# Layer-norm statistics of a transformer block with experts: finishing them once per stage instead of once per tile

## The chip, the cores and the metric

The kernel runs on all 8 cores of one Trainium2 chip. Each core takes half of one of four sequences, 2048 tokens, and does the whole computation for them; the cores exchange nothing. The metric is the device time in microseconds (us) of the slowest core.

## The reference

x has shape (4, 4096, 1024). What is computed, cut to what matters:

```python
h = layernorm(x) * (1 + ca) + sa               # sa, ca, ga, sb, cb, gb from silu(c) @ wmod
a = layernorm(h) * ln1_w + ln1_b
q, k, v = a @ qkv_w.T                          # 16 heads of 64
x1 = h + local_attention(q, k, v) @ proj_w.T   # block of 128 and both neighbours
z = layernorm(x1) * ln2_w + ln2_b
s2 = x + ga * (x1 + gelu(z @ fc1_w.T) @ fc2_w.T)
h2 = layernorm(s2) * (1 + cb) + sb
y = s2 + gb * experts(h2)                      # 8 experts, the best 2 by gate
```

A layer norm needs two numbers per token: the reciprocal standard deviation, and minus the mean times it.

## The kernel before

It is one program of direct engine instructions: every engine has a queue of its own, written in program order, and waits on semaphores by hand (`E.wait`; `waitr` waits relative to the stage's start, `wdma` for a labelled DMA). Tiles are 128 tokens by 1024 features; a core owns 16. The stages follow one another with a barrier between them, at which every engine drains:

1. Modulation vectors from `wmod` (to 227 us of the profile).
2. Two layer norms, the q, k and v projections (to 805).
3. Attention, the output projection, the first residual (805 to 1415). It writes x1, and the residual basis `s_sxa`, to memory and keeps the statistics of x1 in `stats_ln2`, two columns per tile.
4. The MLP (1415 to 2182): 8 groups of two tiles. It reads `stats_ln2`, writes s2, and keeps the statistics of s2 in `stats_s2`.
5. Routing and loading of the experts' weights (to 2447), then the experts (to the end).

**Statistics.** `emit_lnstats` (L233) is called at the end of each tile in stages 3 and 4. VectorE sums the row (L239), ScalarE squares it with an accumulated output (L241, which the trace shows as an ACTIVATE and an accumulator read). Then follow, on columns of one element: VectorE's mean (L245), its square (L250), the variance (L253), plus eps (L257); ScalarE's Ln (L261) and Exp with scale -0.5 (L264); VectorE's product (L268). Each waits for the one before.

**Order in an attention tile.** For each head TensorE makes the scores (L876), ScalarE the exponential with its row sum (L889), TensorE three transposes (L826), VectorE copies them (L831), TensorE multiplies with v (L844). Transposes are written one head behind the scores and the v products two; head 0's transposes wait until two exponentials are done. After 16 heads come the transposes of the output (L909), the projection in two bursts of 8 matmuls (L920) with a bias (L924), VectorE's residual sums (L932, L934, L944, L948) and the statistics. TensorE goes on to the scores of the next tile at once.

**Order in an MLP group.** TensorE runs fc1 in 32 pieces of 8 matmuls (L1143), ScalarE applies gelu to each (L1151), and fc2 (L1122) follows one piece behind. At the end `prep_tile` normalises the next two tiles (L1085 on ScalarE, L1093 and L1097 on VectorE, transposes L1103, copy L1110). Then for each of the group's two tiles VectorE scales the fc2 output (L1174, L1177), adds the residual (L1181), and the statistics follow. The next group's fc1 waits for both tiles' L1181, since it frees the output banks. In the attention and the MLP stage squaring writes its unused result into scratch: `sq_tr2` in attention, `u2_buf` in the MLP, and L1174 writes into `u2_buf` too:

```python
E.wait("tensor", SZTE, SZTE.n)
waitr("tensor", SS2, 2 * g)          # L1134: both tiles of the group before have their sum
```

Of the kernel before, what the change touches and what calls it, by code (L numbers as in the profile page):

```python
# [7 lines left out]
F32 = mybir.dt.float32  # L8
# [8 lines left out]
NT_OWN = 16  # L17
# [67 lines left out]
def build_program(taps=(), nphases=6, a2_tiles=NT_OWN, a2_nopf=99):  # L85
# [633 lines left out]
    if nphases == 2:  # L719
# [16 lines left out]
    ssum = A.alloc("ssum", [128, HEADS], F32)  # L736
    rrb = A.alloc("rrb", [128, HEADS], F32)
    sq_tr2 = A.alloc("sq_tr2", [128, D], F32)
    smA2 = {k: A.alloc(f"smA2_{k}", [128, 1], F32) for k in
            ("s1", "mu", "mu2", "varb", "var", "lnv")}  # L740

    LKVs = [mkdma(f"LKV{i}") for i in range(4)]
    LVVs = [mkdma(f"LVV{i}") for i in range(4)]
# [42 lines left out]
    for t in range(min(NT_OWN, a2_tiles)):  # L786
# [131 lines left out]
        for n in range(2):  # L918
            for k in range(8):
# [44 lines left out]
    if nphases == 3:  # L964
# [166 lines left out]
    for g in range(8):  # L1131
        tiles = (2 * g, 2 * g + 1)
        E.wait("tensor", SZTE, SZTE.n)
        waitr("tensor", SS2, 2 * g)  # L1134
        for m in range(32):
            mu = g * 32 + m
            fb = 2 + (mu % 2)
            if g == 0:
                waitr("tensor", WCM, 8 * (m // 4) + 8)
            waitr("tensor", SGE, mu - 1)  # L1140
            for k in range(8):
                E.op("tensor", lambda e, kk=k, mm=m, b=fb, zt=zT_gr[g % 2]:
                     e.matmul(  # L1143
                         bf(b)[:, 0:256],
                         wfc1_bf[:, kk * DFF + mm * 128: kk * DFF + mm * 128 + 128],
                         zt[:, kk * 256:(kk + 1) * 256],
                         start=(kk == 0), stop=(kk == 7)),
                     inc=SF1.bump() if k == 7 else None)
            E.wait("scalar", SF1, SF1.n)
            waitr("scalar", SF2C, mu - 1)  # L1150
            E.op("scalar", lambda e, mm=m, b=fb, st=tT_r[mu % 2]: e.activation(  # L1151
                st[:, :], bf(b)[:, 0:256], AF.Gelu, bias=fc1b_fm[:, mm:mm + 1]),
                inc=SGE.bump())
            if m >= 1:
                emit_fc2(g, m - 1)
        emit_fc2(g, 31)
        for lt, t in enumerate(tiles):
            ob = obA if lt == 0 else obB
            if g == 0 and lt == 0:
                waitr("tensor", WCB, 1)  # L1160
            for n in range(2):
                E.op("tensor", lambda e, nn=n, b=ob[n]: e.matmul(
                    bf(b)[:, :], ones_bf[0:1, 0:128],
                    fc2b_bf[0:1, nn * 512:(nn + 1) * 512],
                    start=False, stop=True),
                    inc=SF2T.bump() if n == 1 else None)
        if g + 1 < 8:
            prep_tile(2 * g + 2, (g + 1) % 2, 0)
            prep_tile(2 * g + 3, (g + 1) % 2, 1)
        for lt, t in enumerate(tiles):  # L1170
            ob = obA if lt == 0 else obB
            E.wait("vector", SF2T, SF2T.n)
# [523 lines left out]
```

How the kernel before makes its waits and increments, by code:

```python
    def wait(self, eng, sem, val):  # L50
        if val > 0:
            self.on(eng, lambda e, s=sem.h, v=val: e.wait_ge(s, v))
# [1 line left out]
    def op(self, eng, fn, inc=None):  # L54
        if inc is None:
            self.on(eng, fn)
        else:
            sem, k = inc
            self.on(eng, lambda e, f=fn, s=sem.h, kk=k: f(e).then_inc(s, kk))
```

## Time and profile before

| | us |
|---|---|
| timed runs: median of 2 (lowest, highest) | 3000.16 (2999.06, 3001.26) |
| profiled execution, its own time | 2993.95 |
| its span on the slowest core | 2992.4 |
| spans of the 8 cores | 2975.8 to 2992.4 |
| granted TensorE clock, mean of each core | 0.744 to 0.748 |
| busy: TensorE, VectorE, ScalarE, GpSimd | 1799.4, 872.1, 761.7, 70.6 |

The span is the time from a core's first to its last instruction; the execution's time is measured around it. The granted clock is a share of full speed: 0.50 is the lower level (1.2 GHz), 1.00 the upper (2.4 GHz). All cores run the same program and end within 17 us of one another. The rows further down are from core 7, the slowest.

### The profile page before, as it was taken

Reading aid. Unit: us, or ns where it says so; the run is one execution under the profiler, and the core shown is the slowest. Engines: PE = TensorE matmul, PEld = TensorE weight load, DVE = VectorE, ACT = ScalarE, POOL = GpSimd, SP = SyncE. Lnnn points to the kernel's source line nnn. Section 1 sums busy time; section 2 is a strip of 40 time slices with the busy share of each in tenths; the row PEclk is TensorE's granted clock in tenths of the full one; section 3 lists DMA queues with packets and bytes.
Section 4 is the critical chain, followed back from the end, with each engine's and each line's share of the span. In section 5 each row is a group of like instructions: output and inputs, shape, how many; then the busy total and the mean of one; then the engine's idle time right before and its main releaser. Section 6 shows DMA issues by size and latency. Waiting matters only on the chain.

```text
span 2992.4 us, 32560 instructions; the slowest of 8 cores (2975.8 to 2992.4 us)
## 1 busy us (share of the span) xinstructions
PE 1799.4 (60%) x10437; PEld 922.3 (31%) x10437; DVE 872.1 (29%) x1976; ACT 761.7 (25%) x1640; POOL 70.6 (2%) x132
## 2 busy tenths in 40 slices
PE   0411643716666666666344777888721159999999
PEld 0100211202333333333122555555501024444443
DVE  3225133151144444443323221111133321211112
ACT  0103223223122232322101222323233322222222
POOL 0000000000000000000110000000011100000000
PEclk9855866858655555555677888888855569999999
DMA  8251111121422222221664100010046611111110
GB/s 267 72 169 63 60 60 64 57 74 46 148 71 85 71 85 71 71 71 44 187 194 146 43 30 35 36 36 29 33 161 212 213 64 36 53 36 36 36 36 32
DMA packets 108276, 249.39 MB, mean 83 GB/s; under 512 B 30377, under 2 KB 44849, under 8 KB 106062
## 3 DMA queue, kind: packets, MB, share of 16 engines
q1 hardware_dynamic: 69936, 153.42, 16.5%
q10 hardware_dynamic: 27938, 60.33, 5.2%
q0 software_dynamic: 10240, 33.56, 3.4%
q8 instruction: 91, 1.49, 0.2%
q14 instruction: 71, 0.58, 0.1%
HBM read 186.95 MB, written 60.32 MB: 83 GB/s over the span
## 4 chain that ended last, share of the span: by engine, by line
PE 51%; DVE 18%; DMA 12%; ACT 8%; issue 8%; ACTq 1%; DVEq 1%; SPq 0%; PEldq 0%; POOL 0%; PEld 0%; POOLq 0%
PE bank L1552 7%; PE bank L1143 6%; PE bank L1122 6%; PE bank L1566 6%; PE bank L651 5%; DMA arena<-wfc2T 4%; PE bank L920 3%; PE bank L826 3%; PE bank L876 3%; DMA arena<-wmod 2%; DMA arena<-w_in 2%; PE bank L679 2%; ACT arena L241 2%; DVE arena L857 2%; DMA arena<-wqkvT 1%
## 5 line engine op out<-in xcount | busy, mean ns | idle before, releaser
L1143 PE MATMUL bank<-arena 128*128 128x256 bf16 x2048 | 283.7, 286 | 181.4 <-DVE arena L1056 105.0
L1143 PEld LDWEIGHTS bank<-arena 128*128 128x128 bf16 x2048 | 208.2, 102 | 269.6 <-issue 189.5
L1122 PE MATMUL bank<-arena 128*128 128x512 bf16 x1024 | 267.8, 385 | 9.9 <-ACT arena L1151 9.9
L1566 PE MATMUL bank<-arena 128*128 128x512 bf16 x1024 | 244.7, 382 | 3.5 <-DMA arena<-s_h2T 3.5
L1552 PE MATMUL bank<-arena 128*128 128x512 bf16 x1024 | 239.3, 379 | 0.0
L633 PE MATMUL bank<-ident_bf,arena 128*128 128x128 bf16 x144 | 18.2, 306 | 347.3 <-DVE arena L627 347.3
L1151 ACT ACTIVATE arena<-bank,arena 128x256 bf16<-128x256 f32 x256 | 120.8, 475 | 413.7 <-PE bank L1143 413.6
L826 PE MATMUL bank<-ident_bf,arena 128*128 128x128 bf16 x768 | 127.7, 304 | 121.3 <-ACT arena L889 121.1
L241 ACT ACTIVATE arena<-arena 128x1024 f32<-128x1024 f32 x68 | 71.6, 1053 | 486.6 <-DVE arena L948 276.7
L1575 ACT ACTIVATE arena<-bank 128x512 f32<-128x512 f32 x128 | 76.4, 597 | 378.9 <-PE bank L1569 266.4
L1579 DVE TENSOR_SCALAR arena<-arena 128x512 bf16<-128x512 f32 x128 | 62.2, 486 | 376.6 <-ACT arena L1575 376.6
L889 ACT ACTIVATE arena<-bank 128x384 bf16<-128x384 f32 x256 | 125.2, 490 | 154.0 <-PE bank L876 110.6
L651 PE MATMUL bank<-arena 128*128 128x512 bf16 (+1 forms) x640 | 150.4, 383 | 10.1 <-DVE arena L639 5.7
L1566 PEld LDWEIGHTS bank<-arena 128*128 128x128 bf16 x1024 | 97.4, 98 | 125.2 <-issue 16.9
L876 PE MATMUL bank<-arena 64*128 64x128 bf16 x768 | 118.0, 292 | 18.5 <-DMA arena<-q_scr 18.5
L1122 PEld LDWEIGHTS bank<-arena 128*128 128x128 bf16 x1024 | 100.6, 99 | 85.0 <-issue 20.1
L1552 PEld LDWEIGHTS bank<-arena 128*128 128x128 bf16 x1024 | 95.5, 98 | 94.4
L633 PEld LDWEIGHTS bank<-ident_bf,arena 128*128 128x128 bf16 x144 | 13.9, 138 | 353.0 <-issue 353.0
L1093 DVE SCALAR_TENSOR_TENSOR arena<-arena 128x1024 f32<-128x1024 f32 x16 | 19.5, 1220 | 344.1 <-ACT arena L1085 344.1
L1364 PE MATMUL bank<-ident_bf,arena 128*128 128x128 bf16 x128 | 16.2, 305 | 170.4 <-DVE arena L1354 170.4
L826 PEld LDWEIGHTS bank<-ident_bf,arena 128*128 128x128 bf16 x768 | 61.3, 124 | 173.8 <-issue 173.8
L920 PE MATMUL bank<-arena 128*128 128x512 bf16 x256 | 94.1, 533 | 18.4 <-DVE arena L913 18.4
(164 smaller groups left out, 2126.7 us busy)
## 6 DMA issues: line engine op xcount, KB each, us to landing
arena<-wmod SPq DMA_DIRECT2D x16, 1536.0 KB, 8.0
arena<-x_ext SPq DMA_DIRECT2D x34, 512.0 KB, 4.9
arena<-wfc2T POOLq DMA_DIRECT2D x64, 256.0 KB, 4.4
arena<-wfc1T SPq DMA_DIRECT2D x64, 256.0 KB, 4.3
arena<-w_in POOLq DMA_DIRECT2D x64, 256.0 KB, 4.2
arena<-s_s SPq DMA_DIRECT2D x32, 512.0 KB, 5.1
arena<-w_in SPq DMA_DIRECT2D x64, 256.0 KB, 4.9
arena<-wqkvT SPq DMA_DIRECT2D x16, 768.0 KB, 5.5
```

The lines of the kernel that those rows point to most:

```text
L241: E.op("scalar", lambda e: e.activation(sq_trash, X, AF.Square, accum_out=sm["varb"]), inc=sems["SB"].bump())
L651: E.op("tensor", lambda e, kk=k, cw=colw, b=bk, nn=ng: e.matmul(bf(b)[:, 0:nn], wqkv_bf[:, kk * 3072 + cw: kk * 3072 + cw + 128], aT_g[:, ...
L826: e.transpose(bb(b)[:, jj * 128:(jj + 1) * 128], pp[:, jj * 128:(jj + 1) * 128], ident_bf[:, :]),
L876: pr=prow, q0=qcol0, qgb=qg, mk=masked: e.matmul(bf(b)[:, jj * 128:(jj + 1) * 128], qgb[pr:pr + 64, pl * 512 + q0: pl * 512 + q0 + 128], k ...
L889: e.activation(pp[:, :], bf(b)[:, 0:WIN], AF.Exp, accum_out=ssum[:, hh:hh + 1]), inc=SEXP.bump())
L920: E.op("tensor", lambda e, kk=k, nn=n: e.matmul(bf(6 + nn)[:, :], aoT_sb[:, ts(kk, 128)], wproj_bf[:, kk * 1024 + nn * 512: kk * 1024 + nn ...
L1122: st=tT_r[mu % 2]: e.matmul(bf(b)[:, :], st[:, l * 128:(l + 1) * 128], wfc2_bf[:, mm * 1024 + nn * 512: mm * 1024 + nn * 512 + 512], start ...
L1143: e.matmul(bf(b)[:, 0:256], wfc1_bf[:, kk * DFF + mm * 128: kk * DFF + mm * 128 + 128], zt[:, kk * 256:(kk + 1) * 256], start=(kk == 0), s ...
L1151: E.op("scalar", lambda e, mm=m, b=fb, st=tT_r[mu % 2]: e.activation(st[:, :], bf(b)[:, 0:256], AF.Gelu, bias=fc1b_fm[:, mm:mm + 1]), inc= ...
L1552: b=obks[n]: e.matmul(bf(b)[:, :], tT_bf[ii % 3][:, ts(kk, 128)], w2_bf[:, (ee2 * 4 + kk) * 1024 + nn * 512: (ee2 * 4 + kk) * 1024 + nn * ...
L1566: e.matmul(bf(b)[:, :], ht[:, ts(kk, 128)], w1_bf[:, (ee * 8 + kk) * 512:(ee * 8 + kk) * 512 + 512], start=(kk == 0), stop=False))
L1575: E.op("scalar", lambda e, b=bk: e.activation(tE_f[:, :], bf(b)[:, :], AF.Gelu), inc=SGEL.bump())
```

## The change

In stages 3 and 4 a tile now does only its row sum and its squaring, each into a column of its own in buffers of 16 columns. After the last tile the rest is done once over all 16 columns: mean, its square, variance, plus eps, Ln, Exp, product, times -1. Ln and Exp read and write with 16 elements; the outputs go to every second column of `stats_ln2` and `stats_s2`. In the MLP the first instruction of a tile that writes `u2_buf` gets a wait for the squaring of the tile before, and the load of the tile after next waits for one row sum less. In attention ScalarE's squaring waits for the one before on the same engine.

```diff
-    smA2 = {k: A.alloc(f"smA2_{k}", [128, 1], F32) for k in
-            ("s1", "mu", "mu2", "varb", "var", "lnv")}
+    s1A2 = A.alloc("s1A2", [128, NT_OWN], F32)
...
         E.wait("scalar", SX1, SX1.n)
         E.wait("vector", SX1, SX1.n)
-        emit_lnstats(x1_sb[t % 2][:, :], smA2, SLNA2,
-                     stats_ln2[:, 2 * t:2 * t + 1],
-                     stats_ln2[:, 2 * t + 1:2 * t + 2], sq_tr2)
+        E.op("vector", lambda e, tt=t: e.reduce_sum(
+            s1A2[:, tt:tt + 1], x1_sb[tt % 2][:, :], axis=AX.X),
+            inc=SLNA2["SC"].bump())
+        waitr("scalar", SLNA2["SB"], t)
+        E.op("scalar", lambda e, tt=t: e.activation(
+            sq_tr2[:, :], x1_sb[tt % 2][:, :], AF.Square,
+            accum_out=vbA2[:, tt:tt + 1]), inc=SLNA2["SB"].bump())
+
+    _ps = stats_ln2.ap[0][0]
+    stats_ev = bass.AP(stats_ln2.tensor, stats_ln2.offset, [[_ps, 128], [2, 16]])
...
+    E.wait("vector", SLNA2["SB"], SLNA2["SB"].n)
+    E.wait("vector", SLNA2["SC"], SLNA2["SC"].n)
+    E.op("vector", lambda e: e.tensor_scalar(muA2[:, :], s1A2[:, :], INV_D,
+                                             None, ALU.mult), inc=CH2.bump())
+    E.wait("vector", CH2, CH2.n)
+    E.op("vector", lambda e: e.tensor_mul(t1A2[:, :], muA2[:, :], muA2[:, :]),
+         inc=CH2.bump())
...
+    E.wait("scalar", CH2, CH2.n)
+    E.op("scalar", lambda e: e.activation(s1A2[:, :], t1A2[:, :], AF.Ln),
+         inc=CH2.bump())
+    E.wait("scalar", CH2, CH2.n)
+    E.op("scalar", lambda e, ev=stats_ev: e.activation(ev, s1A2[:, :], AF.Exp,
+                                                       scale=-0.5),
+         inc=CH2.bump())
...
             wdma("vector", ("xm", t))
+            waitr("vector", SLNM["SB"], t)
             E.op("vector", lambda e, b=ob[0]: e.scalar_tensor_tensor(
                 u2_buf[:, 0:512], bf(b)[:, :], 1.0, rs(2)[:, 0:512],
                 ALU.mult, ALU.mult))
...
-            emit_lnstats(s2_sb[t % 2][:, :], smM, SLNM,
-                         stats_s2[:, 2 * t:2 * t + 1],
-                         stats_s2[:, 2 * t + 1:2 * t + 2], u2_buf)
+            E.op("vector", lambda e, tt=t: e.reduce_sum(
+                s1M[:, tt:tt + 1], s2_sb[tt % 2][:, :], axis=AX.X),
+                inc=SLNM["SC"].bump())
+            waitr("scalar", SLNM["SB"], t)
+            E.op("scalar", lambda e, tt=t: e.activation(
+                u2_buf[:, :], s2_sb[tt % 2][:, :], AF.Square,
+                accum_out=vbM[:, tt:tt + 1]), inc=SLNM["SB"].bump())
             if t + 2 < NT_OWN:
                 wdma("sync", ("sts2", t))
                 waitr("sync", SLNM["SB"], t + 1)
-                waitr("sync", SLNM["SC"], 5 * t + 1)
+                waitr("sync", SLNM["SC"], t + 1)
```

After the MLP's last tile stands the same chain of eight instructions with `s1M`, `vbM`, `muM`, `t1M` and `stats_s2`.

ScalarE at the end of an attention tile, before. The names give output and input; `arena` is the one buffer in which all on-chip tiles lie, `bank` is PSUM:

```order
L889 ACTIVATE arena<-bank 128x384 x16
L938 DMA s_x<-arena 128x1024
L952 DMA s_sxa<-arena 128x1024
L241 ACTIVATE arena<-arena 128x1024
L261 ACTIVATE arena<-arena 128x1
L264 ACTIVATE stats_ln<-arena 128x1
L889 ACTIVATE arena<-bank 128x384 x16
```

The same place on ScalarE in the changed kernel (its lines stand lower by what was added; L891 is L889 of before, L963 the squaring):

```order
L891 ACTIVATE arena<-bank 128x384 x16
L940 DMA s_x<-arena 128x1024
L954 DMA s_sxa<-arena 128x1024
L963 ACTIVATE arena<-arena 128x1024
L891 ACTIVATE arena<-bank 128x384 x16
```

The Ln and the Exp between the squaring and the next tile's first exponential are gone.

VectorE between the two tiles of an MLP group, before:

```order
L1174 SCALAR_TENSOR_TENSOR arena<-bank,repl 128x512
L1177 SCALAR_TENSOR_TENSOR arena<-bank,repl 128x512
L1181 TENSOR_TENSOR arena<-arena 128x1024
L239 TENSOR_REDUCE arena<-arena 128x1
L245 TENSOR_SCALAR arena<-arena 128x1
L250 TENSOR_TENSOR arena<-arena 128x1
L253 SCALAR_TENSOR_TENSOR arena<-arena 128x1
L257 TENSOR_SCALAR arena<-arena 128x1
L268 TENSOR_SCALAR stats_s<-arena,stats_s 128x1
L1174 SCALAR_TENSOR_TENSOR arena<-bank,repl 128x512
```

The same place on VectorE in the changed kernel (L1215, L1218, L1222 and L1231 are L1174, L1177, L1181 and L239 of before):

```order
L1215 SCALAR_TENSOR_TENSOR arena<-bank,repl 128x512
L1218 SCALAR_TENSOR_TENSOR arena<-bank,repl 128x512
L1222 TENSOR_TENSOR arena<-arena 128x1024
L1231 TENSOR_REDUCE arena<-arena 128x1
L1215 SCALAR_TENSOR_TENSOR arena<-bank,repl 128x512
```

Five instructions on one column, one of which waits for ScalarE, no longer stand between the two tiles.

VectorE at the end of the changed MLP stage, where they come back on 16 columns:

```order
L1231 TENSOR_REDUCE arena<-arena 128x1
L1252 TENSOR_SCALAR arena<-arena 128x16
L1255 TENSOR_TENSOR arena<-arena 128x16
L1258 SCALAR_TENSOR_TENSOR arena<-arena 128x16
L1262 TENSOR_SCALAR arena<-arena 128x16
L1272 TENSOR_TENSOR arena<-arena,stats_s 128x16
L1275 TENSOR_SCALAR stats_s<-arena 128x16
```

They moved from behind each of the 16 tiles to behind the last one; Ln and Exp stand between L1262 and L1272 on ScalarE.

## Rows read from the trace of the kernel before

**Rows 1.** Windows by stage: stretch, length, busy (x instructions) by engine, PEclk, DMA, GB/s.

```profile
805.00:1415.00 610.00, 407.88 (x2753) 216.84 (x2754) 269.17 (x944) 170.65 (x576) 1.20 (x2) 0.57 0.24 77
...
1450.00:2182.00 732.00, 496.30 (x3217) 322.18 (x3218) 159.73 (x301) 182.79 (x350) 31.32 (x58) 0.83 0.23 73
...
2447.00:2993.00 546.00, 529.17 (x2689) 227.98 (x2687) 101.49 (x174) 140.71 (x253) 0.00 (x0) 1.00 0.10 36
```

**Rows 2.** Timeline, attention seam: start, us busy, engine, line, operation [idle before <-releaser].

```profile
849.02 1.21 DVE L239 TENSOR_REDUCE arena<-arena 128x1 f32<-128x1024 f32 x1
...
849.64 1.06 ACT L241 ACTIVATE arena<-arena 128x1024 f32<-128x1024 f32 x1 [16.35 <-DVE arena L948]
...
850.60 0.19 ACT L241 ACTIVATION_READ_ACCUMULATOR arena<-arena 128x1 f32 x1
...
852.14 0.47 ACT L889 ACTIVATE arena<-bank 128x384 bf16<-128x384 f32 x1
...
852.51 0.19 ACT L889 ACTIVATION_READ_ACCUMULATOR arena<-bank 128x1 f32 x1
852.61 0.48 ACT L889 ACTIVATE arena<-bank 128x384 bf16<-128x384 f32 x1
...
852.96 0.48 PE L826 MATMUL bank<-ident_bf,arena 128*128 128x128 bf16 x3 [7.70 <-ACT arena L889]
```

**Rows 3.** Timeline, seam between the first two MLP groups.

```profile
1629.04 0.16 DVE L250 TENSOR_TENSOR arena<-arena 128x1 f32<-128x1 f32 x1 [0.25 <-ACT arena L241]
...
1629.81 1.28 ACT L261 ACT_TABLE_LOAD   x1 [0.93 <-DVE arena L257]
...
1631.10 0.20 ACT L261 ACTIVATE arena<-arena 128x1 f32<-128x1 f32 x1
...
1631.70 0.21 DVE L268 TENSOR_SCALAR stats_s<-arena,stats_s 128x1 f32<-128x1 f32 x1 [1.97 <-ACT stats_s L264]
1631.88 0.69 DVE L1174 SCALAR_TENSOR_TENSOR arena<-bank,repl 128x512 f32<-128x512 f32 x1
...
1634.75 3.31 PE L1143 MATMUL bank<-arena 128*128 128x256 bf16 x16 [10.86 <-DVE arena L1181]
...
1638.91 0.84 ACT L1151 ACTIVATE arena<-bank,arena 128x256 bf16<-128x256 f32 x2
...
1639.53 1.02 PE L1122 MATMUL bank<-arena 128*128 128x512 bf16 x4 [1.47 <-ACT arena L1151]
```

**Rows 4.** Waits before lines L1143 and L1122 on PE, and table loads among ACT's groups.

```profile
  DVE arena L1181: 76.4, 7
...
  ACT arena L1151: 9.9, 8
...
L1151 ACT ACT_TABLE_LOAD x8 | 10.3, 1283 | 18.7 <-PE bank L1143 18.6
L261 ACT ACT_TABLE_LOAD x8 | 10.3, 1283 | 7.5 <-DVE arena L257 7.5
```

**Rows 5.** Timeline at the ends of the attention and the MLP stage.

```profile
1410.09 0.16 DVE L250 TENSOR_TENSOR arena<-arena 128x1 f32<-128x1 f32 x1 [0.44 <-ACT arena L241]
1410.35 0.16 DVE L253 SCALAR_TENSOR_TENSOR arena<-arena 128x1 f32<-128x1 f32 x1
...
2178.36 0.21 DVE L268 TENSOR_SCALAR stats_s<-arena,stats_s 128x1 f32<-128x1 f32 x1 [0.70 <-ACT stats_s L264]
2178.70 0.24 SPq L1265 DMA_DIRECT2D arena<-s_modrow  x1
```

**Rows 6.** Windows behind a TensorE start: two projection bursts, the first MLP seam.

```profile
949.05:954.75 5.70, 5.70 (x13) 1.66 (x14) 0.00 (x0) 0.00 (x0) 0.00 (x0) 0.50 0.53 172
...
1208.33:1211.00 2.67, 2.67 (x7) 1.01 (x8) 0.00 (x0) 0.00 (x0) 0.00 (x0) 0.50 0.13 41
...
1634.75:1637.50 2.75, 2.75 (x14) 1.89 (x15) 1.70 (x5) 1.46 (x4) 0.00 (x0) 0.50 0.46 191
1637.75:1640.75 3.00, 1.53 (x11) 0.77 (x10) 0.17 (x1) 1.99 (x3) 0.00 (x0) 1.00 0.78 265
```

More of the change, by code:

```diff
@@ L738, in build_program @@
     sq_tr2 = A.alloc("sq_tr2", [128, D], F32)
-    smA2 = {k: A.alloc(f"smA2_{k}", [128, 1], F32) for k in
-            ("s1", "mu", "mu2", "varb", "var", "lnv")}
+    s1A2 = A.alloc("s1A2", [128, NT_OWN], F32)
+    vbA2 = A.alloc("vbA2", [128, NT_OWN], F32)
+    muA2 = A.alloc("muA2", [128, NT_OWN], F32)
+    t1A2 = A.alloc("t1A2", [128, NT_OWN], F32)
     LKVs = [mkdma(f"LKV{i}") for i in range(4)]
@@ L956, in build_program @@
         E.wait("vector", SX1, SX1.n)
-        emit_lnstats(x1_sb[t % 2][:, :], smA2, SLNA2,
-                     stats_ln2[:, 2 * t:2 * t + 1],
-                     stats_ln2[:, 2 * t + 1:2 * t + 2], sq_tr2)
+        E.op("vector", lambda e, tt=t: e.reduce_sum(
[7 more added lines that the diff above has]
+    stats_ev = bass.AP(stats_ln2.tensor, stats_ln2.offset, [[_ps, 128], [2, 16]])
+    stats_od = bass.AP(stats_ln2.tensor, stats_ln2.offset + 1,
+                       [[_ps, 128], [2, 16]])
+    E.wait("vector", SLNA2["SB"], SLNA2["SB"].n)
[5 more added lines that the diff above has]
+         inc=CH2.bump())
+    E.wait("vector", CH2, CH2.n)
+    E.op("vector", lambda e: e.scalar_tensor_tensor(
+        t1A2[:, :], vbA2[:, :], INV_D, t1A2[:, :], ALU.mult, ALU.subtract),
+        inc=CH2.bump())
+    E.wait("vector", CH2, CH2.n)
+    E.op("vector", lambda e: e.tensor_scalar_add(t1A2[:, :], t1A2[:, :], EPS),
+         inc=CH2.bump())
+    E.wait("scalar", CH2, CH2.n)
+    E.op("scalar", lambda e: e.activation(s1A2[:, :], t1A2[:, :], AF.Ln),
+         inc=CH2.bump())
+    E.wait("scalar", CH2, CH2.n)
+    E.op("scalar", lambda e, ev=stats_ev: e.activation(ev, s1A2[:, :], AF.Exp,
+                                                       scale=-0.5),
+         inc=CH2.bump())
+    E.wait("vector", CH2, CH2.n)
+    E.op("vector", lambda e, ev=stats_ev: e.tensor_mul(t1A2[:, :], muA2[:, :],
+                                                       ev), inc=CH2.bump())
+    E.wait("vector", CH2, CH2.n)
+    E.op("vector", lambda e, ov=stats_od: e.tensor_scalar(
+        ov, t1A2[:, :], -1.0, None, ALU.mult), inc=CH2.bump())
     for s in STX1s + STSXAs:
@@ L982, in build_program @@
     s2_sb = [A.alloc(f"s2sb{i}", [128, D], F32) for i in range(2)]
-    smM = {k: A.alloc(f"smM_{k}", [128, 1], F32) for k in
-           ("s1", "mu", "mu2", "varb", "var", "lnv")}
+    s1M = A.alloc("s1M", [128, NT_OWN], F32)
+    vbM = A.alloc("vbM", [128, NT_OWN], F32)
+    muM = A.alloc("muM", [128, NT_OWN], F32)
+    t1M = A.alloc("t1M", [128, NT_OWN], F32)
     LWMs = [mkdma("LWMa"), mkdma("LWMb")]
@@ L1199, in build_program @@
                     label=("xm", t + 2))
+    _ps2 = stats_s2.ap[0][0]
+    sts2_ev = bass.AP(stats_s2.tensor, stats_s2.offset, [[_ps2, 128], [2, 16]])
+    sts2_od = bass.AP(stats_s2.tensor, stats_s2.offset + 1,
+                      [[_ps2, 128], [2, 16]])
+    E.wait("vector", SLNM["SB"], SLNM["SB"].n)
+    E.wait("vector", SLNM["SC"], SLNM["SC"].n)
+    E.op("vector", lambda e: e.tensor_scalar(muM[:, :], s1M[:, :], INV_D,
+                                             None, ALU.mult), inc=CHM.bump())
+    E.wait("vector", CHM, CHM.n)
+    E.op("vector", lambda e: e.tensor_mul(t1M[:, :], muM[:, :], muM[:, :]),
+         inc=CHM.bump())
+    E.wait("vector", CHM, CHM.n)
+    E.op("vector", lambda e: e.scalar_tensor_tensor(
+        t1M[:, :], vbM[:, :], INV_D, t1M[:, :], ALU.mult, ALU.subtract),
+        inc=CHM.bump())
+    E.wait("vector", CHM, CHM.n)
+    E.op("vector", lambda e: e.tensor_scalar_add(t1M[:, :], t1M[:, :], EPS),
+         inc=CHM.bump())
+    E.wait("scalar", CHM, CHM.n)
+    E.op("scalar", lambda e: e.activation(s1M[:, :], t1M[:, :], AF.Ln),
+         inc=CHM.bump())
+    E.wait("scalar", CHM, CHM.n)
+    E.op("scalar", lambda e, ev=sts2_ev: e.activation(ev, s1M[:, :], AF.Exp,
+                                                      scale=-0.5),
+         inc=CHM.bump())
+    E.wait("vector", CHM, CHM.n)
+    E.op("vector", lambda e, ev=sts2_ev: e.tensor_mul(t1M[:, :], muM[:, :],
+                                                      ev), inc=CHM.bump())
+    E.wait("vector", CHM, CHM.n)
+    E.op("vector", lambda e, ov=sts2_od: e.tensor_scalar(
+        ov, t1M[:, :], -1.0, None, ALU.mult), inc=CHM.bump())
     for s in STS2s:
```

## The prediction

> **What bounds the kernel now.** I read the table by stage first [rows 1]. It shows no single engine that fills the span. In the attention stage (805 to 1415) TensorE is busy 408 of 610 us at a granted clock of 0.57, hence mostly at the lower of its two levels (1.2 GHz). In the MLP stage (1450 to 2182) it is busy 496 of 732 us at 0.83; in the last, dense one it runs at 1.00 (2.4 GHz). Both stages that the change touches are strings of short dependences, so what counts is which wait ends last at the seam between two units of work. Next I read the timeline at one seam of each stage.
>
> The attention seam is [rows 2]. TensorE has finished the scores of the next tile's first two heads and sits idle 7.70 us, until ScalarE has done two exponentials (L889). These stand in ScalarE's queue behind the statistics of the tile just ended: the squaring (L241) with its accumulator read, then Ln and Exp of one column. Between the start of the accumulator read (850.60) and that of the first L889 (852.14) lie 1.54 us, in which ScalarE works only 0.4 us: it waits for four small VectorE instructions.
>
> The MLP seam is [rows 3]. TensorE idles 10.86 us before the first fc1 matmul of a group, until the residual sum of the second tile (L1181). VectorE starts that tile (L1174) only at 1631.88, since the statistics of the first tile stand in front, and they hold 1.97 us of idle time while ScalarE loads a table (1.28 us) and does Ln and Exp. Then TensorE stops a second time, 1.47 us, for the first gelu (L1151), which had to wait for the second tile's Ln and Exp and for a table load of its own. Both waits recur: 76.4 us in 7 waits for L1181, 9.9 us in 8 waits for L1151, nearly all of it at the same 7 seams; the table loads are 8 for Ln and 8 for gelu [rows 4].
>
> **Attention, per tile.** Removed from ScalarE are Ln and Exp, from VectorE five column instructions; the row sum (L239) and the squaring stay. Behind the accumulator read now stands the first L889. The trace shows this pair in the next head: the read starts at 852.51 and the following L889 at 852.61, 0.10 later [rows 2]. So the first L889 comes at 850.70 instead of 852.14, which is 1.44 us earlier; the worst reading (it starts only when the read has ended) gives 1.3. TensorE's two score blocks are ready long before, and VectorE's L239 ends at 850.23, so neither is late in its place. Next in line is the second L889 and then TensorE's L826, which moves along unchanged. There are 15 such seams: 15 x 1.44 = 21.6 us (bounds 19.5 and 21.6; below that only by a case among the rivals). The reserve of the loads is wide, since keys and values are fetched three tiles ahead.
>
> **End of attention.** The chain now runs once over 16 columns: six VectorE instructions in place of four behind the accumulator read (the mean is now computed here too, and the last product is two instructions), and Ln and Exp. From L250 to L253 is 0.26 us [rows 5], so two more cost 0.5 us. Columns of 16 in place of 1 I take as free, since the fixed part rules at 0.15 us each; the bound is some 0.1 us. It is fully exposed: a stage's last L268 lets the next stage's first load go, as at the end of the MLP (2178.36 and 2178.70).
>
> **MLP seam.** The second tile's L1174 now waits only for the first tile's squaring, because both use u2_buf. L250 waits for that same event today and starts at 1629.04 [rows 3]. L1174 therefore moves from 1631.88 to 1629.04, 2.84 us, and with it L1181 and TensorE's start: 7 x 2.84 = 19.9 us. Behind that new wait on VectorE's queue stand only L1174, L1177 and L1181, which would have come later before. The gelu's gap: with TensorE starting at T, the squaring of the second tile starts beside it and takes 1.25 us with its read (as in [rows 2]), the first eight of the 16 matmuls need half of 3.31 us, so the gelu can start at about T + 1.9 and ends by T + 2.4, while TensorE is busy with the second eight until T + 3.3. With neither Ln, Exp nor a table load in front, the gap goes. At 1.4 us each (7 of them cannot exceed 9.9) it is 9.8 us. The bound on the other side is 0.
>
> **What the clock takes back.** In every seam TensorE restarts at 0.50 and rises later: at the first seam it is still at 0.50 for 2.75 us after the restart and at 1.00 from 3.0 us on [rows 6]. Until now the rise fell on the first 16 matmuls or on the pause behind them. Without the pause, every us that the clock stays low beyond T + 3.4 costs half a us. In the projection bursts of attention the burst starting at 1208.33 is at 0.50 for 2.7 us and the one starting at 949.05 for 5.7 [rows 6], and the rise comes right behind (5.9 at the latest), so I take the middle, 4.3: (4.3 - 3.4) / 2 = 0.45 us, times 7 = 3.2 us back (bounds: 2.5 us gained at 2.7, 8.8 us lost at 5.9).
>
> **End of the MLP.** The last tile starts 2.84 us earlier; the two extra column instructions cost 0.5 us, and the Ln at the end brings a table load that earlier stood at tile 14, 1.28 us. Net gain 1.0 us, exposed as in attention (L268 at 2178.36, next stage at 2178.70) [rows 5]. In the trace a table load costs just its 1.28 us: it begins at 1629.81, as soon as L257's result is there, and Ln follows at its end, 1631.10 [rows 3]. The Trainium skill ("ScalarE: Activation LUTs", section "What ACT_TABLE_LOAD costs") puts a switch at about 2.66 us, load plus a drain as long again. By that rule the net gain here would be an estimated -0.4 us in place of 1.0; the trace does not agree with the drain, and I go by the row.
>
> **Sum.** 21.6 - 0.5 + 19.9 + 9.8 - 3.2 + 1.0 = 48.6 us. The profiled execution took 2993.95 us around a span of 2992.4; the median of the timed runs is 3000.16, 6 us more, and I take the difference off that: 2951.6, rounded 2952. A change of 2% (60 us) is about what a measurement of this kernel can tell from none.
>
> **Rivals.**
> (a) The clock's rises fall well. The gaps between bursts change length everywhere, so the rises move against them. If all came at 2.7 us, 15 projections gain 15 x (4.3 - 2.7) / 2 = 12 us and the MLP another 5.7: 2934. For it: the spread in [rows 6]. Against: it needs luck in every tile; equally, rises near 5.9 cost 12 + 5.6, giving 2970.
> (b) Only one stage pays. If the attention heads wait for something that comes just as late (a load, VectorE), 21 us go: 2973. If in the MLP L1174 gains but the gelu gap merely turns into another, 9.8 us go; if the whole seam does, 2979. Against both: no other wait shows in these seams.
> (c) The change doesn't remove the table loads, because squaring asks for a table of its own between two gelus. Then L1174 comes 1.28 us later than said and the gap stays: 9.0 + 9.8 - 3.2 = 15.6 us less gain, 2967. Against: the squaring at the first tile today follows gelus without a load.
> (d) Slower: the clock fails to come back after the shorter pause, in the MLP. A group between seams is about 53 us of dense work at 1.00 (the stage's mean is 0.83 with seams and weight loading in it [rows 1]); at 1.2 GHz it takes 53 us more. One such group cancels the whole gain, and that is the point from which it decides; two give 2952 + 106 = 3058. For it: in attention the clock stays at 0.57 in the mean though TensorE is busy two thirds of the time. Against: the last stage is denser than the MLP will be, and is granted 1.00 over 546 us [rows 1]. The Trainium skill ("TensorE: Matmul & The Clock Gate", section "What's actually happening" and the notes after it) warns that three or more cores of a die in dense matmuls are held below the full clock; here eight run at once in that last stage, and the trace does not agree.
>
> **How the numbers follow.** Forecast 0.70, own range 2940 to 2965; (a) to the fast side 0.12; (b) 0.12; (c) 0.04; (d) 0.02. The range 2934 to 2974 holds the forecast, (c) and most of (a) and (b). Faster by over 2% (under 2940) is (a) with the edge of the forecast, 0.14; slower is (d), 0.02; within 2% the rest, 0.84.
>
> **What would show it.** The profile after should have the first exponential of a tile 0.1 us behind the accumulator read and a TensorE idle of 6.3 us (not 7.7) at the attention seam; about 8.0 us (not 10.86) at the MLP seam and no second stop before the first fc2; two table loads in the MLP stage in place of 16; and a VectorE row that goes from the row sum to the next L1174 without the 1.97 us. Wrong would be the forecast if the first L889 still starts over 1 us behind the read, if a load or a stop of about 1.4 us remains behind the first 16 matmuls, or if the granted clock of the MLP stage falls below 0.83.

## The result and the profile after

The changed kernel takes 2940.37 us (median of 11 runs) against 2997.5 us (median of 10 runs of the kernel before, measured beside it). The ratio is 0.9817, with a 95% interval of 0.98 to 0.9835: 55 us or 1.8% less. (The medians count every run, also those in which some cores were granted a lower clock than the others; the ratio is of the undisturbed runs alone.) The interval's lower edge lies at 0.98, so whether the change is worth 2% stays open; that it is faster does not. The forecast was 48.6 us less, 2952 us, with a range of its own of 2940 to 2965: the result lies at the fast edge of that range. The profiled execution has spans of 2923.1 to 2937.3 us on its eight cores; their mean fell from 2984.6 to 2930.5, by 54.1 us.

By stage, as the mean over the eight cores (attention starts with its first matmul, every other stage with its first DMA issue). "MLP seams" is from the first to the last residual sum (L1181 of before) of the stage. "Less" is what the change took off:

| stage | before | after | less | forecast |
|---|---|---|---|---|
| attention | 601.4 | 577.3 | 24.1 | 21.1 |
| MLP to its first residual sum | 211.3 | 210.2 | 1.1 | 0 |
| MLP seams | 548.6 | 518.3 | 30.3 | 29.3 |
| behind the last residual sum | 4.8 | 6.7 | -1.9 | -1.8 |
| all else | 1618.5 | 1618.0 | 0.5 | 0 |

(Where the forecast named a "net gain of 1.0 us at the end of the MLP", 2.84 us of it belong to the third row and -1.8 to the fourth.)

Rows of the changed kernel are from core 5, its slowest. The windows of three stages answer to [rows 1]: TensorE's instructions are the same in number, up to a few at the windows' edges, and the stretches are shorter.

```profile
805.00:1391.00 586.00, 403.12 (x2752) 215.84 (x2752) 257.00 (x870) 164.33 (x546) 0.00 (x0) 0.58 0.24 80
1431.00:2127.00 696.00, 501.43 (x3216) 323.96 (x3216) 146.87 (x226) 159.50 (x306) 30.05 (x56) 0.84 0.23 76
2391.00:2937.00 546.00, 529.68 (x2691) 228.21 (x2690) 101.56 (x174) 140.63 (x253) 0.00 (x0) 1.00 0.10 36
```

The attention seam in the timeline answers to [rows 2] (L963 is the squaring, L891 the exponential, L828 the transposes):

```profile
852.59 1.21 DVE L959 TENSOR_REDUCE arena<-arena 128x1 f32<-128x1024 f32 x1
...
853.22 1.06 ACT L963 ACTIVATE arena<-arena 128x1024 f32<-128x1024 f32 x1 [17.21 <-DVE arena L950]
854.18 0.19 ACT L963 ACTIVATION_READ_ACCUMULATOR arena<-arena 128x1 f32 x1
854.27 0.47 ACT L891 ACTIVATE arena<-bank 128x384 bf16<-128x384 f32 x1
...
855.09 0.48 PE L828 MATMUL bank<-ident_bf,arena 128*128 128x128 bf16 x3 [6.25 <-ACT arena L891]
```

The exponential follows the start of the accumulator read by 0.09 us (it was 1.54), and TensorE's stop is 6.25 us (7.70). Over the 120 seams of the eight cores the stop is 6.37 us in the mean, where it was 7.78.

The second MLP seam answers to [rows 3] (L1235 squaring, L1215 the second tile's first instruction, L1183 fc1, L1191 gelu, L1162 fc2):

```profile
1678.12 0.19 ACT L1235 ACTIVATION_READ_ACCUMULATOR arena<-arena 128x1 f32 x1
1678.41 0.69 DVE L1215 SCALAR_TENSOR_TENSOR arena<-bank,repl 128x512 f32<-128x512 f32 x1 [0.49 <-ACT arena L1235]
...
1681.28 3.57 PE L1183 MATMUL bank<-arena 128*128 128x256 bf16 x16 [8.07 <-DVE arena L1222]
1681.59 1.06 ACT L1235 ACTIVATE arena<-arena 128x1024 f32<-128x1024 f32 x1 [3.28 <-DVE arena L1222]
...
1683.30 0.47 ACT L1191 ACTIVATE arena<-bank,arena 128x256 bf16<-128x256 f32 x1 [0.56 <-PE bank L1183]
...
1684.65 1.91 PE L1162 MATMUL bank<-arena 128*128 128x512 bf16 x4
```

TensorE's stop is 8.07 us, and fc2 follows the 16 matmuls with no stop: the gelu started 2.0 us after TensorE did. The waits and table loads answer to [rows 4]:

```profile
  DVE arena L1222: 56.7, 7
...
  ACT arena L1191: 0.5, 1
...
L1191 ACT ACT_TABLE_LOAD x1 | 1.3, 1283 | 19.3 <-PE bank L1183 19.3
...
L1265 ACT ACT_TABLE_LOAD x1 | 1.3, 1283 | 1.3 <-DVE arena L1262 1.3
```

Seven stops of together 56.7 us in place of 76.4: 2.81 us less each, where 2.84 was forecast. The chain at the end of the MLP answers to [rows 5]. It has the steps that were counted, each 0.28 us apart on VectorE:

```profile
2123.26 0.18 DVE L1252 TENSOR_SCALAR arena<-arena 128x16 f32<-128x16 f32 x1 [0.56 <-ACT arena L1235]
2123.54 0.18 DVE L1255 TENSOR_TENSOR arena<-arena 128x16 f32<-128x16 f32 x1
2123.82 0.17 DVE L1258 SCALAR_TENSOR_TENSOR arena<-arena 128x16 f32<-128x16 f32 x1
2124.10 0.17 DVE L1262 TENSOR_SCALAR arena<-arena 128x16 f32<-128x16 f32 x1
2124.36 1.28 ACT L1265 ACT_TABLE_LOAD   x1 [1.27 <-DVE arena L1262]
2125.65 0.22 ACT L1265 ACTIVATE arena<-arena 128x16 f32<-128x16 f32 x1
```

And the clock at that second seam, from TensorE's restart at 1681.28, answers to [rows 6]:

```profile
1681.28:1686.25 4.97, 4.97 (x20) 2.90 (x21) 1.07 (x1) 2.10 (x4) 0.00 (x0) 0.50 0.60 227
1686.50:1688.50 2.00, 2.00 (x16) 1.34 (x15) 0.00 (x0) 0.47 (x1) 0.00 (x0) 0.95 0.90 344
```

It stays at 0.50 for 5 us. The first 16 matmuls take only 3.6 us, and so some dense work now runs at the lower level. That is the term with which the forecast took 3.2 us back.

### The profile page after: what moved, and what is told of

Its sections match the earlier page's. It is cut to its first block, busy times and chain, and to the rows that moved or that the text cites. A ratio compares the mean times of both kernels' runs of the same rounds, so it can differ in the third digit from the quotient of the medians.

```text
span 2937.3 us, 32145 instructions; the slowest of 8 cores (2923.1 to 2937.3 us)
## 1 busy us (share of the span) xinstructions
PE 1801.3 (61%) x10437; PEld 924.3 (31%) x10437; DVE 847.4 (29%) x1828; ACT 732.0 (25%) x1566; POOL 70.3 (2%) x132
## 4 chain that ended last, share of the span: by engine, by line
PE 53%; DVE 17%; DMA 12%; issue 7%; ACT 7%; ACTq 1%; DVEq 1%; SPq 0%; PEldq 0%; POOL 0%; PEld 0%; POOLq 0%
PE bank L1629 8%; PE bank L1183 7%; PE bank L1162 7%; PE bank L1643 6%; PE bank L651 5%; DMA arena<-wfc2T 4%; PE bank L922 3%; PE bank L828 3%; PE bank L878 3%; DMA arena<-wmod 3%; DMA arena<-w_in 2%; PE bank L679 2%; DVE arena L859 2%; DMA arena<-wqkvT 1%; PE bank L846 1%
## 5 line engine op out<-in xcount | busy, mean ns | idle before, releaser
L1183 PE MATMUL bank<-arena 128*128 128x256 bf16 x2048 | 288.5, 289 | 154.8 <-DVE arena L1096 98.1
L1183 PEld LDWEIGHTS bank<-arena 128*128 128x128 bf16 x2048 | 210.4, 103 | 246.7 <-issue 166.3
L1162 PE MATMUL bank<-arena 128*128 128x512 bf16 x1024 | 273.4, 392 | 0.5 <-ACT arena L1191 0.5
L1191 ACT ACTIVATE arena<-bank,arena 128x256 bf16<-128x256 f32 x256 | 121.6, 475 | 423.6 <-PE bank L1183 423.6
L828 PE MATMUL bank<-ident_bf,arena 128*128 128x128 bf16 x768 | 127.6, 304 | 99.8 <-ACT arena L891 99.5
L1652 ACT ACTIVATE arena<-bank 128x512 f32<-128x512 f32 x128 | 76.4, 597 | 378.8 <-PE bank L1646 264.9
L891 ACT ACTIVATE arena<-bank 128x384 bf16<-128x384 f32 x256 | 125.1, 489 | 153.8 <-PE bank L878 111.4
L1162 PEld LDWEIGHTS bank<-arena 128*128 128x128 bf16 x1024 | 102.6, 101 | 76.2 <-issue 11.8
L828 PEld LDWEIGHTS bank<-ident_bf,arena 128*128 128x128 bf16 x768 | 61.2, 124 | 152.4 <-issue 152.4
L894 DVE RECIPROCAL arena<-arena 128x1 f32<-128x1 f32 x256 | 41.8, 163 | 199.5 <-ACT arena L891 199.4
```

The lines of the kernel that those rows point to most:

```text
L828: e.transpose(bb(b)[:, jj * 128:(jj + 1) * 128], pp[:, jj * 128:(jj + 1) * 128], ident_bf[:, :]),
L891: e.activation(pp[:, :], bf(b)[:, 0:WIN], AF.Exp, accum_out=ssum[:, hh:hh + 1]), inc=SEXP.bump())
L1162: st=tT_r[mu % 2]: e.matmul(bf(b)[:, :], st[:, l * 128:(l + 1) * 128], wfc2_bf[:, mm * 1024 + nn * 512: mm * 1024 + nn * 512 + 512], start ...
L1183: e.matmul(bf(b)[:, 0:256], wfc1_bf[:, kk * DFF + mm * 128: kk * DFF + mm * 128 + 128], zt[:, kk * 256:(kk + 1) * 256], start=(kk == 0), s ...
L1652: E.op("scalar", lambda e, b=bk: e.activation(tE_f[:, :], bf(b)[:, :], AF.Gelu), inc=SGEL.bump())
```

## The experiments

All were timed beside the kernel before (medians of 2998.1 and 2999.14 us there). The stage numbers are means over the eight cores of each one's profile. Source lines differ from kernel to kernel; each passage says which are shown.

### One half at a time

`e1_attn_only` changes the attention stage alone, `e2_mlp_only` the MLP stage alone. Against the kernel before, the first has the attention part of the diff shown above and none of the MLP part, and the second the reverse. The first in short:

```diff
-        emit_lnstats(x1_sb[t % 2][:, :], smA2, SLNA2,
-                     stats_ln2[:, 2 * t:2 * t + 1],
-                     stats_ln2[:, 2 * t + 1:2 * t + 2], sq_tr2)
+        E.op("vector", lambda e, tt=t: e.reduce_sum(
+            s1A2[:, tt:tt + 1], x1_sb[tt % 2][:, :], axis=AX.X),
+            inc=SLNA2["SC"].bump())
...
             emit_lnstats(s2_sb[t % 2][:, :], smM, SLNM,
                          stats_s2[:, 2 * t:2 * t + 1],
                          stats_s2[:, 2 * t + 1:2 * t + 2], u2_buf)
```

> Only the attention stage is changed, the MLP stage is that of before. My theory (two independent seams, each paying in its own stage): the attention stage shortens by about 24 us (15 seams of 1.44 us, less 0.5 us for the chain at its end, plus some 3 us from a better placed clock rise), the MLP stage stays at 765 us, the whole is 24 us under before (ratio 0.992). Rival (the gain comes from the MLP stage and the experts' stages alone, the attention heads take back what their first exponential gains): 0 to 5 us.

> Only the MLP stage is changed. My theory: the MLP stage shortens by 27 to 30 us (7 seams of 2.84 + 1.4 us, less what the clock takes back, plus 1 us at the end), attention stays at 601 us, the whole is 27 to 32 us under before (ratio 0.990). Rival (the parts are not additive, one shifts the clock of the other): under 20 us or over 40 us. A second rival for the 3 us by which the stage that loads the experts' weights got shorter in the changed kernel: if it belongs to the change it shows here too, if it is chance it does not.

| kernel | time | ratio (95% interval) | attention | MLP, whole |
|---|---|---|---|---|
| before | 2998.1 | 1 | 601.4 | 764.6 |
| attention alone | 2968.45 | 0.9884 (0.9834 to 0.9934) | 577.1 | 763.9 |
| MLP alone | 2965.05 | 0.9877 (0.9823 to 0.9931) | 601.4 | 737.3 |
| both (the change) | 2940.37 | 0.9817 (0.98 to 0.9835) | 577.3 | 735.2 |

Each half pays in its own stage and leaves the other as it was: 24.3 us and 27.3 us, together 51.6 of the 53.5 us that both stages lose in the changed kernel. The missing 2 us are in the MLP stage's first part, up to the first residual sum (212.7 us with the MLP alone, 210.2 in the changed kernel, and 209.5 to 212.7 over all ten kernels, which hardly differ there); the seams are 518.0 and 518.3 us. The ratios have wide intervals: by them the halves would be worth 35 us (20 to 50) and 37 us (21 to 53). It is the stage times that tell them apart. The rest behind the MLP, in which the loading of the experts' weights seemed 3 us shorter after the change, is 812.9 us before, 810.4 after, 810.2 with attention alone and 811.6 with the MLP alone. In the profiles of the kernels below, whose code is the same there, it is 809.4 to 811.9, and 814.6 in the one that was granted a lower clock at times. It moves by 2.5 us with no change to it, so the difference is not shown to belong to the change.

### What the 1.44 us at the attention seam were

`e4_attn_lnexp` puts a Ln and an Exp back at each tile's end, without their waits:

```diff
             accum_out=vbA2[:, tt:tt + 1]), inc=SLNA2["SB"].bump())
+        E.op("scalar", lambda e: e.activation(
+            dmyA[:, 0:1], dmyA[:, 1:2], AF.Ln))
+        E.op("scalar", lambda e: e.activation(
+            dmyA[:, 2:3], dmyA[:, 3:4], AF.Exp))
```

> The changed kernel with a dummy Ln and a dummy Exp of one column on ScalarE behind each attention tile's squaring, which wait for nothing and for which nobody waits. My theory (most of the 1.44 us was ScalarE waiting for VectorE's four column instructions, only two issue slots of 0.29 us its own work): the first exponential comes 0.6 us later than in the changed kernel, the attention stage is 8 to 9 us longer. Rival 1 (the two instructions themselves are the price): all 21.6 us come back. Rival 2 (the path runs through VectorE and not through ScalarE's queue): 0 to 2 us.

Attention is 580.2 us long, 2.9 us more than in the changed kernel, where 8 to 9 were expected (time 2947.8 us, ratio 0.9818, 0.9767 to 0.987). The timeline of core 5 shows why it is so little (L967 squaring, L970 and L972 the two put back, L895 exponential):

```profile
855.35 0.19 ACT L967 ACTIVATION_READ_ACCUMULATOR arena<-arena 128x1 f32 x1
855.44 0.19 ACT L970 ACTIVATE arena<-arena 128x1 f32<-128x1 f32 x1
855.53 0.19 ACT L972 ACTIVATE arena<-arena 128x1 f32<-128x1 f32 x1
855.62 0.47 ACT L895 ACTIVATE arena<-bank 128x384 bf16<-128x384 f32 x1
```

Before, on core 7, the same two stood like this:

```profile
851.74 0.20 ACT L261 ACTIVATE arena<-arena 128x1 f32<-128x1 f32 x1 [0.95 <-DVE arena L257]
852.03 0.20 ACT L264 ACTIVATE stats_ln<-arena 128x1 f32<-128x1 f32 x1
```

Two instructions that wait for nothing take 0.09 us each in ScalarE's queue, 0.18 us per seam and 15 x 0.18 = 2.7 us in all. So 1.26 of the 1.44 us were ScalarE standing still for VectorE's columns and for its own Ln. The theory holds in kind; its size was wrong, since it took the 0.29 us from the Ln to the Exp of before, of which the second waits for the first, as the price of an instruction. By the stage time alone rival 2 (0 to 2 us, a path through VectorE) is not far off; what speaks against it is the place: TensorE's first transposes start 0.18 us later behind the start of the projection's last matmul (7.27 us against 7.09 in the mean of 120 seams), as much as the queue grew.

### What a table load costs at the MLP seam

`e3_mlp_tableload` makes ScalarE leave gelu's table once per group:

```diff
                 accum_out=vbM[:, tt:tt + 1]), inc=SLNM["SB"].bump())
+            if lt == 1:
+                E.op("scalar", lambda e: e.activation(
+                    dmyM[:, 0:1], dmyM[:, 1:2], AF.Exp))
```

> The changed kernel with one dummy Exp of one column on ScalarE behind the second tile's squaring of each MLP group; nobody waits for it. It brings back the two table loads per seam and nothing else. My theory (the table loads stood on the path only in front of the first gelu): a second stop of TensorE of 1.2 to 1.5 us comes back at each of 7 seams, the first stop stays at 8.1 us; 9 us at most, and 4 to 5 us where the stop falls into the time in which the clock is low anyway. Rival 1 (table loads are hidden beside the 16 matmuls): 0. Rival 2 (a load drags a drain with it, 2.7 us for each): stops of about 4 us, over 20 us in all.

The MLP seams take 529.4 us, 11.1 us more than in the changed kernel. The time of the whole is 2963.33 us, the ratio 0.984 (0.9755 to 0.9924). It is not used further: outside the MLP stage the profiled execution has stretches at a third granted clock, 0.81, which no other profile here shows. They are the last 94 and 101 us of cores 6 and 7, and on cores 4 and 5 two each of 37 to 55 us, near 310 and 430 us. On core 7, with the clock third from the end:

```profile
2840.00:2850.00 10.00, 10.00 (x54) 4.38 (x53) 0.97 (x2) 2.72 (x6) 0.00 (x0) 1.00 0.13 50
2860.00:2950.00 90.00, 90.00 (x383) 35.93 (x382) 13.29 (x23) 19.27 (x35) 0.00 (x0) 0.81 0.06 21
```

The waits of lines L1187 (fc1) and L1166 (fc2) on core 5:

```profile
  DVE arena L1226: 56.7, 7
...
  ACT arena L1195: 10.8, 8
```

The first stop is untouched (56.7 us), the second is back (10.8 us in 8 waits, against 0.5 in one). Rival 1 is out. So is rival 2, that a drain comes with each load: over all 56 seams a stop is 1.3 to 2.0 us, 1.55 in the mean. But the 11.1 us are above the 9 us that the theory allowed at most, and it had expected the clock to give part of it back: a stop that falls into time at the lower level costs only half its length in work at full speed. It gave nothing back. At the first seam of core 5 (L1187 fc1, L1166 fc2):

```profile
1621.54 3.57 PE L1187 MATMUL bank<-arena 128*128 128x256 bf16 x16 [8.23 <-DVE arena L1226]
1626.43 1.86 PE L1166 MATMUL bank<-arena 128*128 128x512 bf16 x4 [1.32 <-ACT arena L1195]
1628.09 1.91 PE L1187 MATMUL bank<-arena 128*128 128x256 bf16 x8
1629.80 1.41 PE L1166 MATMUL bank<-arena 128*128 128x512 bf16 x4
1631.05 1.04 PE L1187 MATMUL bank<-arena 128*128 128x256 bf16 x8
```

Eight matmuls of fc1 take 1.91 us in the dense stretch here and 1.04 later, so the clock came up only some 9 us after the restart. Seam by seam, over the 7 seams of each of the eight cores (us; "clock up" is the time from TensorE's restart until the granted clock is 1.00):

| kernel | first stop | clock up: mean | range | over 7 us |
|---|---|---|---|---|
| before | 10.91 | 3.92 | 2.7 to 8.9 | 4 of 56 |
| after | 8.10 | 4.94 | 2.6 to 6.0 | 0 of 56 |
| with table loads | 8.10 | 4.86 | 2.6 to 9.4 | 18 of 56 |

The mean is the same with the table loads as without, but the rises fall into two groups: 38 come at 2.6 to 3.3 us, before the second stop, which then costs its whole length; at the other 18 TensorE enters the stop (3.6 us after the restart) at the lower level, and the rise comes only at 7.8 to 9.4. Without the second stop no rise came later than 6.0 us, in any of the 392 seams of the seven kernels here that lack it. So a short second stop that comes before the rise can put it off by some 3 us. It doesn't always: in the kernel before, 25 rises fell into the stop itself (3.6 to 4.3 us) and only 4 were put off. Why 38 rises come earlier than in the changed kernel isn't shown.

### The wait that the change added, and what else holds the MLP seam

`e5_mlp_ownbuf` takes the shared buffer away, and with it the new wait:

```diff
-            waitr("vector", SLNM["SB"], t)
...
-                u2_buf[:, :], s2_sb[tt % 2][:, :], AF.Square,
+                sqM[:, :], s2_sb[tt % 2][:, :], AF.Square,
```

`e6_mlp_sums_last` also issues both tiles' row sums behind the second residual sum:

```diff
             E.wait("vector", SS2, SS2.n)
-            E.op("vector", lambda e, tt=t: e.reduce_sum(
-                s1M[:, tt:tt + 1], s2_sb[tt % 2][:, :], axis=AX.X),
-                inc=SLNM["SC"].bump())
+            if lt == 1:
+                for tq in tiles:
+                    E.op("vector", lambda e, tt=tq: e.reduce_sum(
+                        s1M[:, tt:tt + 1], s2_sb[tt % 2][:, :], axis=AX.X),
+                        inc=SLNM["SC"].bump())
```

> The changed kernel, but squaring in the MLP writes its unused result into a bf16 buffer of its own, so that the second tile's first instruction needs no wait for it. My theory (the new wait costs the 0.49 us that VectorE idles between the row sum and the next tile): 8 x 0.49 = 4 us less between the first and the last residual sum of the MLP stage. Rival (the wait is hidden behind something else): 0.

> As the one with its own buffer, and both tiles' row sums stand behind the second tile's residual sum. My theory (TensorE's stop at the MLP seam is VectorE's queue, instruction by instruction): 1.7 us less at each of the 8 group ends, 13 to 14 us less between the first and the last residual sum, 1.2 us more behind the last one; TensorE's stop falls from 8.1 to 6.4 us. Rival (loads or ScalarE then end last): the stop stays over 7.5 us.

| kernel | time | ratio (95% interval) | stop | clock up: mean | MLP seams | behind them |
|---|---|---|---|---|---|---|
| after | 2940.37 | 0.9817 (0.98 to 0.9835) | 8.10 | 4.94 | 518.3 | 6.7 |
| own buffer | 2938.48 | 0.9794 (0.9767 to 0.9822) | 7.48 | 4.05 | 510.0 | 6.7 |
| sums last | 2922.6 | 0.9748 (0.9731 to 0.9765) | 6.49 | 3.59 | 500.5 | 7.4 |

The waits of L1184 (fc1) for L1222 (the residual sum) on each one's slowest core, with the own buffer and then with the sums last:

```profile
  DVE arena L1222: 52.4, 7
```

```profile
  DVE arena L1222: 45.4, 7
```

The stop falls by 0.6 and by 1.6 us, as VectorE's queue says. The gains (8.3 and 17.8 us) are both 4 us above what was expected. In both the clock comes up earlier after the restart, 0.89 and 1.35 us, which at half a us saved for each us of rise and 7 seams is 3.1 and 4.7 us. The trace settles that the surplus is the clock's: from the restart to the first transposes at the group's end TensorE does the same matmuls with no stop over 0.2 us in all three kernels, and that stretch is 59.16 us in the mean after, 58.74 with the own buffer and 58.48 with the sums last, 0.42 and 0.68 us less or 2.9 and 4.8 us at 7 seams. In time alone the own buffer can't be told from the change.

### Attention: the work behind the first exponentials

`e7_attn_late` keeps the change but issues the two stores, the row sum and the squaring behind head 3 of the next tile:

```diff
+        def late(t=t, a=sx1n, b=ssxan):
+            E.wait("scalar", SX1, a)
+            dma("scalar", lambda e, tt=t: e.dma_start(
+                s_x1[tt, :, :], x1_sb[tt % 2][:, :]), STX1s[t % 2],
+                label=("stx1", t))
+            E.wait("scalar", SSXA, b)
...
+            E.op("vector", lambda e, tt=t: e.reduce_sum(
+                s1A2[:, tt:tt + 1], x1_sb[tt % 2][:, :], axis=AX.X),
+                inc=SLNA2["SC"].bump())
+            waitr("scalar", SLNA2["SB"], t)
...
+            if h == LATE_H and late_box:
+                late_box.pop()()
```

`e8_both` has this and the sums last of `e6_mlp_sums_last`.

> The changed kernel, but in attention the two stores, the row sum and the squaring of a tile are issued behind head 3 of the next tile. My theory (what is left of TensorE's stop at the attention seam is ScalarE's queue until the squaring, then VectorE's residual chain): the first exponential comes about 5 us earlier, the first transposed copy on VectorE about 2.5 to 3 us earlier, and the displaced work costs about 1 us inside the heads; attention 20 to 30 us shorter. Rival 1 (the heads are full, the displaced work costs there what it cost at the seam): 0 to 5 us. Rival 2 (the clock: the shorter stop keeps it up, or its rises fall worse): over 35 us, or slower.

> The last two together. If both stages are independent, as the two halves of the change were, it gains the sum: 33 to 43 us under the changed kernel (about 2895 to 2905 us). Rival (one of them loses in the other's company): less than the larger of the two alone.

| kernel | time | ratio (95% interval) | attention | MLP, whole |
|---|---|---|---|---|
| attention late | 2916.02 | 0.9725 (0.9674 to 0.9775) | 543.2 | 734.1 |
| attention late and sums last | 2899.65 | 0.9662 (0.9638 to 0.9687) | 543.9 | 720.5 |

Attention loses another 34.1 us, more than the 20 to 30 expected. The seam on core 1, the slowest (L880 scores, L893 exponential, L830 transposes, L951 the residual's last sum, L835 the copy, L848 the products with v, L969 squaring):

```profile
852.75 0.35 PE L880 MATMUL bank<-arena 64*128 64x128 bf16 x6
...
853.19 0.49 ACT L893 ACTIVATE arena<-bank 128x384 bf16<-128x384 f32 x1 [12.60 <-PE bank L880]
...
854.02 0.33 PE L830 MATMUL bank<-ident_bf,arena 128*128 128x128 bf16 x3 [0.92 <-ACT arena L893]
...
855.72 1.22 DVE L951 TENSOR_TENSOR arena<-arena 128x1024 f32<-128x1024 f32 x1
...
857.58 0.25 PE L848 MATMUL bank<-arena 128*128 128x64 bf16 x3 [2.69 <-DVE arena L835]
...
859.31 1.06 ACT L969 ACTIVATE arena<-arena 128x1024 f32<-128x1024 f32 x1 [0.37 <-issue]
```

The exponential now waits only for the scores. TensorE's stops are 0.92 and 2.69 us in place of one of 6.25; the second is VectorE's residual chain.

Where the 34.1 us come from can be read over all 120 seams. Counted from the start of the projection's last matmul, the first copy of transposes (L835) comes after 4.68 us, where it was 7.69: 3.0 us earlier, the upper end of what was expected. The first product with v comes 3.06 us earlier. The displaced work makes the stretch from there to the transposes of the output 0.74 us longer (19.86 against 19.12), and not 1 us. That is 15 x (3.06 - 0.74) = 34.8 us; the projection bursts, 0.07 us longer each, take 1.1 back. The first transposes also run at the upper level of the clock at all 120 seams (0.33 us for three, where it was 0.48), but they stand before the stop that VectorE ends, so nothing shows that this shortens the seam. Rival 1 is out. Rival 2 named over 35 us; its mechanism is not needed for what was measured.

Both together take the mean span from 2930.5 to 2886.1, 44.4 us less, against 33.6 and 19.1 alone. In the two stages it is 48.1 us, nearly the sum of 34.1 and 17.0; the MLP seams give 2.0 us less than alone. The other 3.7 us were lost in stages that no edit touches. In time it is the fastest kernel here.

## Why the prediction was right

The forecast was 48.6 us less and the result is 55 by the ratio, 54.1 by the mean spans. Of the 5.5 us between 48.6 and 54.1, 3.0 are in attention, 1.0 at the MLP seams, 1.1 in the MLP's first part and 0.5 in stages that the change doesn't touch. By the forecast's steps:

- **Attention, 21.6 us.** The place and the size hold: the first exponential stands 0.09 us behind the read, TensorE's stop is 1.45 us shorter, and with attention alone the stage pays in full. The stage lost 3 us more than forecast. A projection burst (L920 and L924) takes, from its first matmul to its second bias, 5.88 us in the mean of 128 bursts, where it took 6.16: 16 x 0.28 = 4.5 us. The work is the same; the clock comes up 4.2 us after a burst's start in the mean, where it was 4.8 (on the six cores whose bursts are recorded whole). The forecast had set that term to zero and kept it as case (a). Against it stand small losses: the first product with v comes 1.39 us earlier at a seam and not 1.44, each tile gives back 0.05 us further on, and the stage's end costs 0.7.
- **End of attention and of the MLP, 0.5 and 1.8 us lost.** 0.7 us measured in attention (from the last residual sum to the next stage's first load 4.20 us, it was 3.54), 1.9 us at the MLP. An instruction of 16 columns takes 0.17 to 0.18 us, one of a single column 0.15 to 0.16, so the width was nearly free, as taken. The table load cost its 1.28 us, 2124.36 to 2125.65, and Ln stood right at its end: the drain of the Trainium skill ("ScalarE: Activation LUTs", section "What ACT_TABLE_LOAD costs") does not show here either.
- **MLP seam, 2.84 us each.** TensorE's stop is 2.81 us shorter at each of 7 seams. The new wait costs what was said: VectorE idles 0.49 us in it.
- **The gelu's gap, 1.4 us each.** Gone at every seam. The run with the table loads brings back a gap of that size (1.55 us) with one small Exp that waits for nothing, and so shows that it was the table and not the chain of Ln and Exp. (The forecast gave the squaring with its read 1.25 us; by [rows 2] it is 1.15, and it ends before the gelu either way.)
- **What the clock takes back, 3.2 us.** Mis-sized. The rise comes 4.94 us after the restart in the mean, not 4.3, so the term is 7 x (4.94 - 3.4) / 2 = 5.4 us. The stretch from the restart to the first transposes at the group's end agrees: it fell from 59.88 to 59.16 us, and so only half of the 1.4 us came through. Two things that the forecast did not have go the other way. The second stop itself had put the rise off past 8 us at 4 of 56 seams before. And at the seams after the first, TensorE's first eight transposes, which stand on VectorE's path, ran at the lower level before and run at the upper one now: the first row is of before (core 7), the second of after (core 5).

```profile
1696.52 1.01 PE L1103 MATMUL bank<-ident_bf,arena 128*128 128x128 bf16 x8 [1.97 <-DVE arena L1097]
```

```profile
1668.01 0.61 PE L1143 MATMUL bank<-ident_bf,arena 128*128 128x128 bf16 x8 [1.97 <-DVE arena L1137]
```

That is 0.4 us at a seam and 2.4 us at six of them; over all cores they ran at the upper level at 3 of 48 such seams before and at 48 of 48 after. With it 22.7 + 9.8 - 5.4 + 2.4 = 29.5 us against 30.3 measured in the third row of the stage table (22.7 is 2.84 at eight pairs of tiles). That the forecast's 29.3 for this row came so close is in part luck: 2.2 us too little for the clock and 2.4 us left out cancel.

Of the rivals, (b), one stage not paying, is out by the two halves alone. (c), a table for the squaring, is out by the two table loads. (d), a clock that fails to come back, did not happen: the stage's mean is 0.84. (a), the rises falling well, is part of the surplus: they fell better in attention (4.2 us after a burst's start, not 4.8) and worse in the MLP (4.94 after the restart, not 3.92). A granted clock below full in the dense last stage, which (d) weighed, did not show before or after the change; one profile, that of the kernel with the table loads, has it: 0.81 on cores 6 and 7 for the last 94 and 101 us.

## What to carry to other kernels

A handful of one-column instructions that hand results back and forth between two engines costs little work and much standing still: 1.26 of 1.44 us per tile in attention. What decides its price is the instruction queued behind it on either engine, so look there first, and keep only what must be per tile. Moving whole instructions off the seam (the squaring behind the next tile's first exponentials, row sums behind the last residual) took another 44.4 us off the mean span, on top of the change's 54.1, at no saving in work.

## What the runs showed of the hardware

- Instructions on ScalarE that wait for nothing follow each other by 0.09 us for one column, while a pair of which the second waits for the first needed 0.29 (L261 and L264 of before).
- TensorE's clock makes small moves in time count or not. After a stop of 8.1 us it came up anywhere from 2.6 to 6.0 us after the restart, though the stop and the matmuls were the same at each seam; with table loads that put a second stop of 1.3 to 2.0 us behind the first 16 matmuls it came at 2.6 to 3.3 or at 7.8 to 9.4. A short stop can therefore cost as much as its length even where part of it falls into time at the lower level (11.1 us for 10.8 us of stops), and shortening the main stop by 0.6 us gained 1.2 us per seam.
- A third level of the granted clock, 0.81, was seen in one of the ten profiles, on two cores at a time. In the other nine all eight cores were granted 1.00 in the last stage, in dense matmuls.
